# VectorE's order at the entry to SwiGLU and in each group's first units

## What is computed

```python
x = _layernorm(x + _L0_attn_ref(x, ...))
x = _layernorm(x + _L0_ffn_ref(x, ...))
```

## Time and profile before

| | us |
|---|---|
| median of 3 executions (755.73 to 756.63) | 755.79 |
| the profiled execution | 758.11 |
| its span, first to last instruction | 756.3 |
| TensorE (PE) busy | 731.0 (97%) |
| VectorE (DVE) busy | 474.7 (63%) |
| ScalarE (ACT) busy | 212.4 (28%) |
| GpSimd (POOL) busy | 156.8 (21%) |
| mean granted TensorE clock | 0.995 of full speed |

### The profile page before, as it was taken

One profiled execution on the slowest core, in us unless ns is written; L12 is line 12 of the kernel. 1 busy time (PEld: TensorE's weight loads), 2 busy tenths in 40 slices (PEclk: granted clock), 3 DMA queues, 4 the chain that ended last, 5 costly groups with the idle time before them and its releaser, 6 DMA issues.

```text
span 756.3 us, 12165 instructions
## 1 busy us (share of the span) xinstructions
PE 731.0 (97%) x3431; PEld 332.4 (44%) x3431; DVE 474.7 (63%) x916; ACT 212.4 (28%) x340; POOL 156.8 (21%) x132
## 2 busy tenths in 40 slices
PE   5999999999999999999999999999999999999994
PEld 2444443444444444444444444444444444444442
DVE  4787677697777779488867779653755371124115
ACT  1644357444712121211112121222122212222210
POOL 0433452211111111111111111221122212222120
PEclk9999999999999999999999999999999999999998
DMA  9438309410000000110001532004020006001001
GB/s 320 180 96 279 55 3 331 112 56 1 1 14 16 15 17 0 21 22 15 1 15 23 105 68 45 16 16 98 0 70 15 0 2 153 0 1 56 0 1 55
DMA packets 35364, 43.37 MB, mean 57 GB/s; under 512 B 19974, under 2 KB 27782, under 8 KB 34438
## 3 DMA queue, kind: packets, MB, share of 16 engines
q1 hardware_dynamic: 33222, 38.78, 17.3%
q0 software_dynamic: 2112, 4.19, 3.5%
HBM read 34.33 MB, written 4.44 MB: 51 GB/s over the span
## 4 chain that ended last, share of the span: by engine, by line
PE 79%; DVE 10%; issue 4%; ACT 3%; DMA 2%; SPq 1%; DVEq 1%; ACTq 0%; POOL 0%
PE acc L453 27%; PE pb L439 18%; PE pa L439 18%; PE acc L518 9%; DVE work L1225 1%; DMA big<-in_x_t 1%; PE acc L736 1%; PE pick_a L501 1%; DVE big L1349 1%; DVE small L1242 1%; DVE big L1334 1%; DVE big L1332 1%; DVE big L1031 1%; DVE big L1336 1%; ACT big L879 1%
## 5 line engine op out<-in xcount | busy, mean ns | idle before, releaser
L453 PE MATMUL acc<-big,work 128*128 128x512 f16 (+1 forms) x1104 | 248.4, 379 | 0.0
L940 POOL TENSOR_TENSOR work<-work 128x512 f32 (+1 forms) x96 | 113.2, 1183 | 512.2 <-ACT work L859 283.8
L439 PE MATMUL pb<-xs,big 128*128 128x512 f16 (+1 forms) x816 | 187.2, 379 | 4.5 <-DVE work L1225 4.2
L439 PE MATMUL pa<-xs,big 128*128 128x512 f16 (+1 forms) x816 | 189.1, 379 | 2.2 <-ACT work L854 1.1
L453 PEld LDWEIGHTS acc<-big,work 128*128 (+1 forms) x1104 | 107.8, 98 | 129.2 <-issue 3.6
L439 PEld LDWEIGHTS pb<-xs,big 128*128 128x128 f16 (+1 forms) x816 | 78.1, 98 | 97.7 <-issue 7.4
L439 PEld LDWEIGHTS pa<-xs,big 128*128 128x128 f16 (+1 forms) x816 | 77.8, 98 | 92.9 <-issue 4.0
L917 ACT ACTIVATE work<-work 128x512 f32 x56 | 35.2, 628 | 220.1 <-DVE work L1454 217.0
L518 PE MATMUL acc<-big 128*128 128x512 f16 x336 | 73.7, 379 | 0.6 <-POOL big L947 0.6
L1454 DVE SCALAR_TENSOR_TENSOR work<-big,const_sb,pa 128x512 f32<-128x512 f16 (+1 forms) x28 | 20.9, 745 | 83.2 <-PE pa L439 82.9
L859 ACT ACTIVATE work<-work 128x512 f32 (+1 forms) x40 | 25.2, 630 | 167.0 <-DVE work L1225 167.0
(11 more groups left out here) (140 smaller groups left out, 517.7 us busy)
## 6 DMA issues: line engine op xcount, KB each, us to landing
big<-in_w_all SPq DMA_DIRECT2D x2, 3840.0 KB, 17.0
big<-spread_rows SPq DMA_DIRECT2D x16, 448.0 KB, 6.9
big<-in_x_t SPq DMA_DIRECT2D x16, 256.0 KB, 4.1
rows<-in_x POOLq DMA_DIRECT2D x4, 1024.0 KB, 10.4
big<-in_w_all SPq DMA_DIRECT2D x2, 1536.0 KB, 10.8
out<-rows SPq DMA_DIRECT2D x3, 1024.0 KB, 4.6
big<-in_w_all SPq DMA_DIRECT2D x1, 2048.0 KB, 17.5
big<-in_w_all SPq DMA_DIRECT2D x2, 1024.0 KB, 5.5
```

The source lines that it names most:

```text
L439: mm = nc.tensor.matmul(dst[:, :], weights(wp)(kc * P, P), x_part16(g, xp, kc), start=(kc == 0 and wp == xp), stop=(kc == KC - 1 and wp == 1))
L453: mm = nc.tensor.matmul(acc[t][:, :], act_part(pair, j, ap, t * P, P), weights(wp)(0, H), start=(first and ap == wp), stop=(last and ap == 1))
L940: nc.gpsimd.tensor_tensor(act_part(pair, j, 1), act32[j], act_part(pair, j, 0), ALU.subtract).then_inc(act_lo, 1)
```

## The change

In words, by place:

- **Taylor, group 3** (TensorE, `group_peaks`): the peak of w1's maximum is taken behind term 4, not term 5, waiting for the 18 terms of three groups instead of 24.
- **Entry** (VectorE): the low halves of chunk 0 come before the four small operations on the scales, which signal `gate_scaled`, for which ScalarE now waits ahead of its first SiLU; in unit u of group 0 the SwiGLU product goes before the low halves of W1_BEFORE_UP. ScalarE copies the last Taylor sums in two pairs, one behind each product of unit 0, instead of four behind the second.
- **w2's plan**: the fourth slot has four chunks instead of five, the seventh two instead of one.
- **First units of groups 2 and 3**: in unit 0 the fourth pick is left out, and done behind unit 1's second SwiGLU product. Unit 1 of group 1 has its first SwiGLU product before the moments; in groups 2 and 3 it stays behind them.
- **First tile**: `normalise(..., low=tile)` issues `x1_low(tile)` behind the second of the four normalised rows, in groups 1 to 3 and in phase 2's first two groups, where it stood behind the second SwiGLU product, or at the head of the next unit.

```diff
@@ -264,6 +264,7 @@
         w1_hi, w2_hi = sem("w1_hi"), sem("w2_hi")
         x1_hi, c1_hi = sem("x1_hi"), sem("c1_hi")
 
+        gate_scaled = sem("gate_scaled")
         act_lo, peak_ready, term_lo = sem("act_lo"), sem("peak_ready"), sem("term_lo")
         fuse_lo = sem("fuse_lo")
 
@@ -282,7 +283,7 @@
         W1_BEFORE_UP = {(0, 0): (2, 3), (0, 1): (3, 4), (1, 0): (4, 5), (1, 1): (5, 6), (2, 0): (6, 7), (2, 1): (7, 8), (3, 0): (9, 10)}
         W1_AFTER_UP = {(2, 1): (8, 9)}
         W2_PIECES = ((2, 5), (5, 8), (8, 12), (0, 2), (12, C2))
-        W2_PLAN = (0, 1, 3, 4, 9, 10, 12, 13, C2)
+        W2_PLAN = (0, 1, 3, 4, 8, 9, 11, 13, C2)
         N1 = GROUPS * C1
 
 
@@ -474,8 +475,8 @@
                     peaks(1, [t_part[:, 1:2]], delta_bank(0))
                 elif g == 0 and m == G:
                     peaks(PEAK_X1, [x_part[:, 1:2], c1_part], u_bank(0))
-                elif g and m == (0, 5, 4, 5)[g]:
-                    pe.wait_ge(terms_ready, (g + 1) * G)
+                elif g and m == (0, 5, 4, 4)[g]:
+                    pe.wait_ge(terms_ready, min(g + 1, GROUPS - 1) * G)
                     if g + 1 < GROUPS:
                         peaks(g + 2, [x_part[:, g + 1:g + 2], t_part[:, g + 1:g + 2]], delta_bank(g))
                     else:
@@ -771,9 +772,9 @@
                 act.activation(delta_size, delta_bank(g)[:, :], ACT.Abs, bias=point_sb[:, 0:1]).then_inc(delta_sized, 1)
                 act.activation(delta_bank(g)[:, :], delta_bank(g)[:, :], ACT.Identity, bias=point_sb[:, 0:1]).then_inc(delta_ready, 1)
 
-            def copy_sums(g):
-
-                for t in range(TPG):
+            def copy_sums(g, tiles=range(TPG)):
+
+                for t in tiles:
                     act.wait_ge(taylor_ready, g * TPG + t + 1)
                     act.activation(rows[:, g * TPG + t, :], acc[t][:, :], ACT.Copy, scale=t_inv[:, g:g + 1]).then_inc(sum_copied, 1)
 
@@ -841,6 +842,7 @@
             act.wait_ge(w_scaled, 1)
             w1_high(0, W1_BEFORE)
             act.activation(silu_first, disc_sb[:, 0:1], ACT.Silu)
+            act.wait_ge(gate_scaled, 1)
 
 
             def swiglu(g, u, start=False, tile=None, slots=None):
@@ -887,8 +889,8 @@
                             w1_high(*W1_BEFORE_UP[u, j])
                     elif (u, j) in W1_AFTER_UP:
                         w1_high(*W1_AFTER_UP[u, j])
-                    elif (u, j) == (0, 1):
-                        copy_sums(3)
+                    elif u == 0:
+                        copy_sums(GROUPS - 1, range(2 * j, 2 * j + 2))
                     if u == U1 - 1:
                         prepare_w2(2 * j + at)
                 return go
@@ -1041,9 +1043,10 @@
                 dve.wait_ge(x_scaled, GROUPS)
                 settle()
 
-                step(v.tensor_scalar(gate_out, x_inv, w_inv[:, 0:1], None, ALU.mult))
+                v.tensor_scalar(gate_out, x_inv, w_inv[:, 0:1], None, ALU.mult).then_inc(gate_scaled, 1)
                 step(v.tensor_scalar(up_out, x_scale, w_scale[:, 0:1], 2.0 ** -59, ALU.mult, ALU.mult))
                 settle()
+                dve.wait_ge(gate_scaled, 1)
                 step(v.scalar_tensor_tensor(out=spare, in0=gate_out, scalar=2.0 ** 59, in1=gate_out, op0=ALU.mult, op1=ALU.mult))
                 settle()
                 step(v.tensor_scalar(down_out, spare, w_inv[:, 0:1], None, ALU.mult))
@@ -1215,8 +1218,9 @@
             settle()
             v.tensor_reduce(w_part[:, 0:1], w1_part_max, axis=AX.X, op=ALU.max).then_inc(max_part, 1)
             scale_phase1()
+            w1_low(0, 1)
             scale_phase1_sums()
-            w1_low(0, W1_BEFORE)
+            w1_low(1, W1_BEFORE)
 
             def swiglu(g, u, j):
                 n = g * C1 + u * 2 + j
@@ -1240,12 +1244,14 @@
                     dve.wait_ge(banks_added, added(phase, g, t))
                     apart(dve, vector_passed)
                     step(v.bn_stats(stats[:, t, :], row(g, t)))
+                if not tiles:
+                    return
                 settle()
                 apart(dve, vector_passed)
                 for t in tiles:
                     step(v.bn_aggr(mv[:, t, :], stats[:, t, :]))
 
-            def normalise(g, signal, tiles=range(TPG)):
+            def normalise(g, signal, tiles=range(TPG), low=None):
 
                 at = slice(tiles[0], tiles[-1] + 1)
                 ve_, y_, ya_ = ve[:, at], y[:, at], ya[:, at]
@@ -1278,6 +1284,8 @@
                 for t in tiles:
                     v.tensor_scalar(row(g, t), row(g, t), mv[:, t, 0:1], y[:, t:t + 1],
                                     ALU.subtract, ALU.mult).then_inc(signal, 1)
+                    if t == 1 and low is not None:
+                        x1_low(low)
 
             CUBE = 3.0 / 8.0
             NORM_STEPS = 2 * TPG + 3 + 7
@@ -1373,13 +1381,13 @@
 
             for u in range(U1):
                 for j in range(2):
-                    if (u, j) in W1_BEFORE_UP:
-                        w1_low(*W1_BEFORE_UP[u, j])
                     if u == U1 - 1:
                         if j == 0:
                             scale_phase2()
                         w2_low(W2_PLAN[2 * j], W2_PLAN[2 * j + 1])
                     swiglu(0, u, j)
+                    if (u, j) in W1_BEFORE_UP:
+                        w1_low(*W1_BEFORE_UP[u, j])
                     if (u, j) in W1_AFTER_UP:
                         w1_low(*W1_AFTER_UP[u, j])
                     if (u, j) == (0, 0):
@@ -1417,17 +1425,23 @@
                 pick(tile, 1, pick_b)
                 pick(tile, 2, pick_a)
                 swiglu(g, u, 1)
-                pick(tile, 3, pick_b)
+                if nxt is not None:
+                    pick(tile, 3, pick_b)
 
             TILE_STEPS = Z_STEPS + PICKS * PICK_STEPS - 1
 
-            def group1(g):
-
-                moments(g - 1, 1)
+            def first_unit1(g, last=None, ahead=range(TPG), behind=()):
+
+                moments(g - 1, 1, ahead)
                 swiglu(g, 1, 0)
-                normalise(g - 1, x1_ready)
+                moments(g - 1, 1, behind)
+                normalise(g - 1, x1_ready, low=g * TPG - TPG)
                 swiglu(g, 1, 1)
-                x1_low(g * TPG - TPG)
+                if last is not None:
+                    pick(last, 3, pick_b)
+
+            def tile_units1(g):
+
                 with steps.loop(2, U1, TILE_STEPS) as u:
                     unit1(g, u, (g - 1) * TPG + (u - 2), (g - 1) * TPG + (u - 1))
 
@@ -1435,11 +1449,13 @@
             for g in range(GROUPS):
                 dve.wait_ge(rows_in[g], 16)
             take(0, down_ready, down_out[:, 0:1])
+            first_unit1(1, ahead=(), behind=range(TPG))
             with steps.loop(1, GROUPS - 1, NORM_STEPS + TPG * TILE_STEPS) as g:
-                group1(g)
+                tile_units1(g)
                 unit1(g + 1, 0, g * TPG - 1)
                 take(g, down_ready, down_out[:, bass.ds(g, 1)])
-            group1(GROUPS - 1)
+                first_unit1(g + 1, g * TPG - 1)
+            tile_units1(GROUPS - 1)
 
 
             def mask_hidden(g, u):
@@ -1464,21 +1480,19 @@
             take(GROUPS - 1, down_ready, down_out[:, GROUPS - 1:GROUPS])
             pick(tile, 2, pick_a)
 
-            def first_unit(g, tile, phase, signal):
+            def first_unit(g, tile, phase, signal, low=None):
 
                 settle()
                 mask_hidden(g, 1)
                 if tile is not None:
                     pick(tile, 3, pick_b)
                 moments((g - 1) % GROUPS, phase)
-                normalise((g - 1) % GROUPS, signal)
+                normalise((g - 1) % GROUPS, signal, low=low)
 
             for g in range(2):
-                first_unit(g, g * 2 + ((GROUPS - 1) * TPG - 1), (1, 2)[g], (x1_ready, rows_out)[g])
+                first_unit(g, g * 2 + ((GROUPS - 1) * TPG - 1), (1, 2)[g], (x1_ready, rows_out)[g], g * 2 + (GROUPS - 1) * TPG)
                 for i in range(2):
                     tile = g * 2 + ((GROUPS - 1) * TPG + i)
-                    if i == 0:
-                        x1_low(tile)
                     mask_hidden(g, 2 * i + 2)
                     cut_z(tile, pick_a)
                     mask_hidden(g, 2 * i + 3)
```

## The result

The changed kernel takes 748.29 us (median of 5 executions, 748.11 to 748.62); the kernel before, 756.60 in 5 executions beside it and in those behind the forecast (755.73 to 758.06). The ratio is 0.9891, 95% interval 0.988 to 0.9902: 8.3 us, or 1.1%, faster. I had forecast 746.1. The measured time lies outside the range of that forecast alone (745.2 to 747.5), and inside the wide one (744.3 to 749.5), which takes in three of the rivals.

A forecast was written before the change was run, and what follows sets the result against it. TensorE was taken as the bound, full from 446 to 740 us and before that waiting mainly for VectorE's SwiGLU product. 2.68 + 0.94 + 3.50 + 2.69 - 0.1 = 9.7 us off 755.79 gives 746.1, range 745.2 to 747.5 (0.60).

The forecast's parts named there:

- Part 1: Entry: earlier w1 maximum, SwiGLU product before low halves, split copies of last sums remove four TensorE waits, 2.68 us.
- 3 x 0.69: Entry, VectorE: three low halves of 0.69 us each, so a SwiGLU product put before them comes 2.07 earlier.
- spare 0.2 to 0.4: Behind the entry: margin in us by which VectorE's weight maxima would end before TensorE wants their peak.
- The pair that was to fit with 5.16 in 5.18: Entry: VectorE's tightest pair, with the low half of x, takes 5.16 us against two TensorE products' 5.18.
- the entry is bound elsewhere: Rival, chance 0.14: VectorE's pair or maxima come late, the entry's gain is given back at w2's peak; 748.8 us.
- Part 2: w2's plan: one chunk moved behind group 1's first SwiGLU product removes two TensorE waits, 0.94 us.
- Part 3: Groups 1 to 3: later fourth pick, or SwiGLU before moments in group 1, removes three TensorE waits, 3.50 us.
- Part 4: First tile's low half between normalised rows: 2.69 us from groups 2, 3 and phase 2; group 1 0.1 worse.
- 1.2 earlier: Group 2, first tile: low half ends 2.25 us after the first row's start, against 3.44 before.
- The ring: Rival, chance 0.03: at the entry VectorE and ScalarE wait for each other in series, 4.3 lost per pair; 766.1 us.
- the clash of waits in the first units: Rival, chance 0.11: wait between rows or moved pick ends late, half of parts 3 and 4 lost; 749.2 us.
- Weight loads: First-tile turns: if always pulled ahead, three turns give about 0.9 instead of 2.69, the whole change about 8 us.

The follow-up runs named there:

- the two kernels that bring back the 2.79: Changed kernel with VectorE's group loop begun by unit 1's second SwiGLU product, 747.81 us; and with a small copy there, early w2 maxima and tile 0 first, 745.65.

## Why the prediction was right, and where it was not

- **The sum.** 9.7 forecast, 8.37 in the trace: the places and the mechanism were right, two sizes were not (0.67 at w2's peak, 0.7 in the loop). The median was missed by 2.2 us: 1.3 by the sum, and 0.8 because I subtracted from a median of three executions, 755.79, which more executions put at 756.0 to 756.6.
- **Part 1, size.** The entry gave its 2.68 within 0.01 (0.48 + 2.19). The step that failed is the term "3 x 0.69" for the low halves: behind a SwiGLU product they take 2.96. The earlier trace rows could not show it, but the row at 125.07 of the same trace did. The "spare 0.2 to 0.4" for VectorE's maxima was counted with 2.07, and would have been about 0.4; 0.9 more used it up. The pair that was to fit with 5.16 in 5.18 took 5.82 (products at 118.62 and 124.44), and TensorE did not wait: the second of them was done at 125.18, and TensorE's next up product began at 126.19. The rival "the entry is bound elsewhere" named the place, w2's peak, but would have given back 2.68; it was 0.67. That early maxima remove it is shown. The causes that I gave to the three edits are not confirmed: singly they are worth 0.68, 0.15 and 0.04, and at least two of them cover for each other.
- **Part 2.** The waits went, as forecast. But the term is not worth 0.94 in this kernel: with the plan back, 0.30 is lost, since group 1's turn takes up the rest. My sum missed nothing by this, as it had charged group 1 with TensorE's lead.
- **Part 3.** The three waits (3.5 us) are gone, and the pick's new place costs nothing. What I had left out, a term put at nothing, is the loop: 0.11 in each of six units, 0.7 in all. This is the failed term of groups 1 and 2; turning the loop shows it.
- **Part 4.** The turns of groups 2 and 3 closed whole, group 1's didn't (4.26, forecast 4.3), phase 2's stretch fell by 0.39 where I had 0.40 (luck in part: my window began 0.16 late, so the loss before was 0.50, and 0.11 of it stays). The step "1.2 earlier" was right (2.27 behind the first row's start, forecast 2.25), the attribution was not: part 3 alone closes the turns of groups 2 and 3. In group 1 part 4 is worth 1.3 us of wait, and in the profiled execution 1.5 of clock.
- **The ring, and the clash of waits in the first units** did not occur: no wait on w1's low halves and none at z's split is in the trace.
- **Weight loads.** The windows decided rightly against a price of the printed wait alone: the three turns gave 1.32 + 0.96 + 0.39 = 2.67, forecast 2.69, where weight loads that are always ahead would have given about 0.9. That this change as a whole came near the "about 8" of that case (8.37) has the two causes above. The stretch without a printed wait, which still lost 0.81, shows it once more.

## What to carry to other kernels

Before you price an edit by the wait that it removes, ask which other edit, or which slack, already covers the same wait; take the parts back one by one and together, for two parts can be doubles (here parts 3 and 4), or an earlier arrival can only move the wait to the next place (part 2). An operation put directly behind another one inherits what that one sets off on other engines: here a subtraction on GpSimd, with which three low halves took 0.9 us longer. And when a loop's body is turned, look at the register operations on the engine's queue, which no busy time shows.

## What was unexpected of the hardware

- In one profile a wait of 1.60 us on TensorE, with eight small matmuls behind it, was followed by 4 us at a granted clock of 0.61, which cost 1.54 us. Waits of 2.01 us between two full products, and of 0.3 before the small matmuls, left it at 1.00.
- A stretch with eight small matmuls whose input comes just in time cost 0.81 us more than elsewhere, though no wait is printed.
- The same VectorE instructions answered TensorE 0.11 us later in a loop whose head does not use the outer loop's value first. That register work is what delays them is argued from the one register operation (64 to 71 ns) before each of the six late products, which is gone in the two kernels that bring back the 2.79; how it gets there, and how 64 ns become 110, stays open.
- The first stretch, with the same code, took from 23.65 to 26.42 us in the profiled executions.
